# Four of twelve blocks of attention probabilities, turned by VectorE and transfers instead of by TensorE

## What is computed

```python
x = x + 0.5 * ffn(layernorm(x), w_gate, w_up, w_down)
x = x + attn(layernorm(x), gamma, w_qkv, w_out)
x = x + 0.5 * ffn(layernorm(x), w_gate, w_up, w_down)

# ffn:  silu(x @ w_gate.T) * (x @ w_up.T) @ w_down.T, 1024 hidden columns
# attn: rows scaled to unit norm, * 16 * gamma; 16 query heads, 4 key/value heads of 64,
q, k = rotary(q), rotary(k)
sim = einsum('bihd,bjhd->bhij', q / 8, k)        # causal mask
out = einsum('bhij,bjhd->bihd', softmax(sim), v) @ w_out
```

## Time and profile before

| | us |
|---|---|
| median of 3 runs | 595.22 (594.51 to 595.42) |
| the profiled execution | 594.24 |
| its span, first to last instruction | 592.4 |

### The profile page before, as it was taken

The page is one execution under the profiler, slowest core; times in us unless marked ns, Lnnn a source line. Parts: engine busy times, 40 slices in busy tenths (PEclk is TensorE's granted clock), DMA queues, the critical chain, the costliest instruction groups (busy, mean ns, idle before and its releaser), DMA issues.

```text
span 592.4 us, 13551 instructions
## 1 busy us (share of the span) xinstructions
PE 560.4 (95%) x4308; PEld 525.4 (89%) x4308; DVE 435.9 (74%) x1302; ACT 395.0 (67%) x1045; POOL 382.4 (65%) x368
## 2 busy tenths in 40 slices
PE   6889988999999999999999999999999999988997
PEld 2877777989999999999999999999999999777897
DVE  4768886859867795868867695868867696888632
ACT  3564993479736895379826896379926896379722
POOL 0666772887739765696838875686838875476523
PEclk9999998999999999999999999999999999989999
DMA  7410000350006200260005300170004400000000
GB/s 251 141 69 3 1 1 20 83 131 2 19 19 156 56 18 0 62 169 0 18 18 134 79 18 0 41 189 0 18 18 116 96 0 0 18 2 2 1 18 19
DMA packets 28089, 29.68 MB, mean 50 GB/s; under 512 B 2976, under 2 KB 25888, under 8 KB 28064
## 3 DMA queue, kind: packets, MB, share of 16 engines
q1 hardware_dynamic: 28064, 29.37, 19.0%
HBM read 8.39 MB, written 2.10 MB: 18 GB/s over the span
## 4 chain that ended last, share of the span: by engine, by line
PE 59%; ACT 13%; issue 10%; DVE 8%; SPq 5%; POOL 3%; DMA 1%; POOLq 0%; DVEq 0%; ACTq 0%
PE bank L928 40%; PE bank L937 7%; PE bank L1049 5%; ACT probs L528 5%; PE bank L1027 4%; SPq L273 3%; PE bank L1023 2%; SPq L262 2%; ACT hid L555 1%; DVE hid L812 1%; PE bank L923 1%; ACT xn L464 1%; DVE rope_s L700 1%; ACT o_sums L540 1%; DMA q_t<-rotated 1%
## 5 line engine op out<-in xcount | busy, mean ns | idle before, releaser
L381 POOL TENSOR_TENSOR probs<-probs,inv_sum 128x512 f32<-128x512 f32 (+1 forms) x64 | 94.0, 1470 | 43.7 <-DVE inv_sum L789 43.5
L528 ACT ACTIVATE probs<-probs,neg_max 128x128 f32<-128x128 f32 (+1 forms) x256 | 113.1, 450 | 1.6 <-DVE neg_max L779 1.6
L390 POOL TENSOR_TENSOR hid_lo<-hid,hid_hi 128x512 fp32r<-128x512 f32 x64 | 83.8, 1314 | 22.4 <-ACT hid_hi L563 21.6
L928 PE MATMUL bank<-xf_t_hi,gate_hi 128*128 128x256 f32 x256 | 75.2, 294 | 5.3 <-DVE hid L812 2.1
L928 PE MATMUL bank<-down_hi,hid_hi 128*128 128x256 f32 x256 | 72.6, 283 | 1.9 <-POOL hid_lo L390 1.9
L928 PE MATMUL bank<-xf_t_hi,up_hi 128*128 128x256 f32 x256 | 72.1, 282 | 0.0
L400 POOL TENSOR_TENSOR o_t_lo<-o_sums,o_t_hi 128x512 fp32r<-128x512 f32 x32 | 41.8, 1305 | 46.7 <-ACT o_t_hi L547 46.6
L928 PE MATMUL bank<-xf_t_lo,gate_hi 128*128 128x256 f32 x256 | 71.6, 280 | 0.0
L928 PE MATMUL bank<-xf_t_hi,gate_lo 128*128 128x256 f32 x256 | 71.6, 280 | 0.0
L928 PE MATMUL bank<-down_lo,hid_hi 128*128 128x256 f32 x256 | 71.4, 279 | 0.0
L928 PE MATMUL bank<-down_hi,hid_lo 128*128 128x256 f32 x256 | 71.4, 279 | 0.0
(11 more groups left out here) (128 smaller groups left out, 1896.5 us busy)
## 6 DMA issues: line engine op xcount, KB each, us to landing
q_t<-rotated SPq DMA_DIRECT2D x96, 128.0 KB, 2.7
k_t<-rotated_k SPq DMA_DIRECT2D x48, 128.0 KB, 2.7
x_in<-in_x SPq DMA_DIRECT2D x7, 256.0 KB, 2.8
out<-y_out SPq DMA_DIRECT2D x7, 256.0 KB, 2.1
probs<-in_w_qkv SPq DMA_DIRECT2D x4, 384.0 KB, 3.3
probs<-in_w_gate SPq DMA_DIRECT2D x2, 512.0 KB, 6.0
probs<-in_w_up SPq DMA_DIRECT2D x2, 512.0 KB, 6.9
probs<-in_w_down SPq DMA_DIRECT2D x2, 512.0 KB, 5.7
```

The costliest lines, as they stand in the source:

```text
L381: nc.gpsimd.tensor_tensor(part, part, inv_sum[:, slot].unsqueeze(2).broadcast_to([P, GROUP, keys]), ALU.mult).then_inc(p_done, 1)
L390: nc.gpsimd.tensor_tensor(hid_lo[:, slot].rearrange("p c n -> p (c n)"), hid[:, slot], hid_hi[:, slot].rearrange("p c n -> p (c n)").bitca ...
L528: last = nc.scalar.activation(part, part, ACT.Exp, bias=neg_max[:, slot, g:g + 1], scale=-1.0, accum_out=row_sum[:, slot, g:g + 1])
L928: last = nc.tensor.matmul(dst, a[x], b[y], start=start and i == 0, stop=stop and i == 2, skip_group_check=shared)
```

## The change

In the loop, the blocks of key block 0 of groups 4, 5, 6 and 7 (`TURNED`) take another way. VectorE turns each with one instruction that transposes every 32x32 square (`turn_blocks`), into one of two halves of a new buffer `turned`; SyncE issues four transfers for it (`z_restack`), each of which takes 32 partitions of `turned` to all 128 partitions of the low part's buffer, 512 bytes for each; ScalarE copies the block from there to the high part's buffer (`turned_hi`), and VectorE subtracts that in place (`turned_lo`). SyncE's transfers of group n wait for the turned block and for `values(n - 2)`.

The columns of a block then lie by row square, head and row in it. The eight blocks that TensorE still transposes in the loop are written to the bank in the same arrangement (`by_rows`), and `small_half` and `add_large_half` put the sums back in the order of the heads (`head_order`). `values` multiplies key block 1 first and waits for each block by itself. The opening and the ending keep their transposes.

The lists of the loop are new on all engines. They hold the same calls as before, in another order, but for the new ones and those that they replace.

```diff
-TRANSPOSES = dict(opening=22, turn=15, ending=20)
+BLOCK = 32
+TURNED = [(4, 0), (5, 0), (6, 0), (7, 0)]
+TRANSPOSES = dict(opening=22, turn=15 - len(TURNED), ending=20)
...
-        sb("under_rotated_k", [P, 2, 2, SEQ])
+        turned = sb("turned", [P, 2, P // BLOCK, GROUP * BLOCK])
...
+        def head_order(turn, part, bank_order=False):
+
+            if turn.now is None:
+                return part
+            if bank_order:
+                return part.rearrange("p (a g q) -> p a g q", a=P // BLOCK, g=GROUP)
+            return part.rearrange("p (g a q) -> p a g q", a=P // BLOCK, g=GROUP)
...
+        z_ready, z_hi, z_lo = (sig(n, len(TURNED)) for n in ("z_ready", "z_hi", "z_lo"))
+        z_in = [sig(f"z_in{i}", 16 * (P // BLOCK)) for i in range(len(TURNED))]
...
+            def z_restack():
+
+                m = c["Z"]
+                n, kb = TURNED[m]
+                sp.wait_ge(z_ready, turn.at(z_ready, m + 1))
+                sp.wait_ge(rope_sum, turn.at(rope_sum, NT * ROW_JOBS + QK_JOBS))
+                if n > 1:
+                    sp.wait_ge(o_ready, turn.at(o_ready, GROUPS + n - 1))
+                for a in range(P // BLOCK):
+                    sp.dma_start(p_t[n % 2][1][:, kb, a * P:a * P + P].bitcast(F32),
+                                 turned[BLOCK * a:BLOCK * a + BLOCK, m % 2]).then_inc(z_in[m], 16)
+                c["Z"] += 1
...
-                k_restack(0), q_restack(0), k_restack(1), q_restack(1), k_restack(2), q_restack(2), k_restack(3)
-                q_restack(3), x_load(), y_store()
+                k_restack(0), k_restack(1), q_restack(0), q_restack(1), q_restack(2), k_restack(2), k_restack(3)
+                q_restack(3), z_restack(), z_restack(), x_load(), z_restack(), z_restack(), y_store()
...
+            def turned_hi(n, kb):
+
+                m = TURNED.index((n, kb))
+                act.wait_ge(z_in[m], turn.at(z_in[m], 16 * (P // BLOCK)))
+                nc.scalar.activation(p_t[n % 2][0][:, kb], p_t[n % 2][1][:, kb].bitcast(F32), ACT.Copy
+                                     ).then_inc(z_hi, 1)
...
-                nc.scalar.activation(o_sums[rows], bank[O_BANK][other], ACT.Copy).then_inc(o_small, 1)
+                nc.scalar.activation(head_order(turn, o_sums[rows]), head_order(turn, bank[O_BANK][other], True), ACT.Copy
+                                     ).then_inc(o_small, 1)
...
+            def turn_blocks(n, kb):
+
+                m = TURNED.index((n, kb))
+                dve.wait_ge(p_done, turn.at(p_done, GROUPS + n + 1))
+                if m == 0:
+                    for j in range(KV_HEADS):
+                        dve.wait_ge(k_in[j], turn.at(k_in[j], 16 * 2))
+                if m > 1:
+                    dve.wait_ge(z_in[m - 2], turn.at(z_in[m - 2], 16 * (P // BLOCK)))
+                nc.vector.transpose(turned[:, m % 2].rearrange("p b (g q) -> p g b q", g=GROUP),
+                                    probs[:, n % 4, :, kb * P:kb * P + P].rearrange("p g (k b) -> p g b k", b=P // BLOCK)
+                                    ).then_inc(z_ready, 1)
+
+            def turned_lo(n, kb):
+
+                dve.wait_ge(z_hi, turn.at(z_hi, TURNED.index((n, kb)) + 1))
+                rest = p_t[n % 2][1][:, kb]
+                nc.vector.tensor_tensor(rest, rest.bitcast(F32), p_t[n % 2][0][:, kb].bitcast(F32), ALU.subtract
+                                        ).then_inc(z_lo, 1)
...
+                sums = head_order(turn, o_sums[rows])
+                nc.vector.tensor_tensor(sums, sums, head_order(turn, bank[O_BANK][rows], True), ALU.add).then_inc(o_sum, 1)
...
-                first_statistics(), rope_products(0), rope_products(1), row_shift(), second_statistics(x2)
-                rope_products(2), x_lo(xf_t), rope_lo(0), rope_lo(1), rope_products(3), gate_product(), up_product()
-                rope_products(4), gate_product(), up_product(), gate_product(), row_shift(), up_product()
-                mask_max(0), mask_max(1), value_halves(), mask_max(0), mask_max(1), inverse(), gate_product()
-                x_lo(xf_t), up_product(), mask_max(0), inverse(), mask_max(1), mask_max(0), p_lo(0, 0), inverse()
-                mask_max(1), gate_product(), mask_max(0), mask_max(1), inverse(), p_lo(1, 0), add_large_half(0)
-                mask_max(0), inverse(), mask_max(1), add_large_half(1), up_product(), p_lo(2, 0), gate_product()
-                p_lo(3, 0), mask_max(0), up_product(), inverse(), mask_max(1), add_large_half(2), p_lo(4, 1)
-                mask_max(0), p_lo(4, 0), ffn_residual(x1_next, x_in), inverse(), gate_product(), add_large_half(3)
-                p_lo(5, 1), p_lo(5, 0), mask_max(1), up_product(), attention_statistics(), inverse()
-                add_large_half(4), p_lo(6, 1), p_lo(6, 0), add_large_half(5), gate_product(), up_product()
-                p_lo(7, 1), add_large_half(6), p_lo(7, 0), row_shift(True), add_large_half(7), x_lo(xa_t)
-                ffn_residual(y_out, x2), attention_residual(x2, 0), attention_residual(x2, 1)
+                first_statistics(), rope_products(0), row_shift(), rope_products(1), rope_products(2)
+                second_statistics(x2), x_lo(xf_t), rope_lo(0), rope_lo(1), row_shift(), rope_products(3)
+                gate_product(), up_product(), rope_products(4), gate_product(), up_product(), gate_product()
+                mask_max(0), mask_max(1), up_product(), value_halves(), mask_max(0), mask_max(1), gate_product()
+                up_product(), inverse(), x_lo(xf_t), mask_max(0), mask_max(1), inverse(), inverse(), p_lo(0, 0)
+                mask_max(0), mask_max(1), gate_product(), up_product(), mask_max(0), inverse(), p_lo(1, 0)
+                mask_max(1), add_large_half(0), p_lo(2, 0), mask_max(0), mask_max(1), inverse(), add_large_half(1)
+                gate_product(), mask_max(0), mask_max(1), turn_blocks(4, 0), ffn_residual(x1_next, x_in), inverse()
+                add_large_half(2), up_product(), p_lo(3, 0), mask_max(0), turn_blocks(5, 0), p_lo(4, 1), inverse()
+                add_large_half(3), gate_product(), turned_lo(4, 0), mask_max(1), up_product(), turn_blocks(6, 0)
+                inverse(), p_lo(5, 1), add_large_half(4), turned_lo(5, 0), p_lo(6, 1), turn_blocks(7, 0)
+                attention_statistics(), add_large_half(5), turned_lo(6, 0), p_lo(7, 1), gate_product(), up_product()
+                add_large_half(6), turned_lo(7, 0), row_shift(True), add_large_half(7), ffn_residual(y_out, x2)
+                x_lo(xa_t), attention_residual(x2, 0), attention_residual(x2, 1)
...
+                    to = t_bank(c)[:, i * P:i * P + P]
+                    if by_rows:
+                        to = t_bank(c)[:].rearrange("p (a g q) -> p a g q", a=P // BLOCK, g=GROUP)[:, :, i]
+                    last = nc.tensor.transpose(to, block_in, eye_sb[:])
...
-                pe.wait_ge(t_lo, turn.at(t_lo, c[f"p{n % 2}"]))
                 if n == 0:
                     pe.wait_ge(v_done, turn.at(v_done, c["V"]))
                 else:
                     pe.wait_ge(o_sum, turn.at(o_sum, c["O"]))
-                for kb in range(t + 1):
+                for kb in range(t, -1, -1):
+                    if turn.now is not None and (n, kb) in TURNED:
+                        pe.wait_ge(z_lo, turn.at(z_lo, TURNED.index((n, kb)) + 1))
+                    else:
+                        pe.wait_ge(t_lo, turn.at(t_lo, c[f"p{n % 2}"]))
                     for s in range(2):
                         last = nc.tensor.matmul(bank[O_BANK][:], v_halves[:, kb, j], p_t[n % 2][s][:, kb],
-                                                start=kb == 0 and s == 0, stop=kb == t and s == 1)
+                                                start=kb == t and s == 0, stop=kb == 0 and s == 1)
...
-                gate(), scores(0), scores(1), up(), down(), scores(0), gate(), scores(1), up(), x_transposes("ff")
-                scores(0), down(), scores(1), down(), scores(0), gate(), scores(1), p_transposes(0, 0)
-                p_transposes(1, 0), up(), scores(0), values(0), scores(1), gate(), scores(0), scores(1)
-                p_transposes(2, 0), values(1), down(), p_transposes(3, 0), scores(0), scores(1), up(), values(2)
-                p_transposes(4, 1), p_transposes(4, 0), gate(), scores(0), values(3), up(), scores(1)
-                p_transposes(5, 1), p_transposes(5, 0), down(), values(4), p_transposes(6, 1), p_transposes(6, 0)
-                gate(), up(), values(5), down(), p_transposes(7, 1), p_transposes(7, 0), values(6), projection(0, 0)
-                down(), values(7), projection(0, 1), down(), x_transposes("xa"), projection(1, 0), projection(1, 1)
+                gate(), scores(0), scores(1), up(), down(), scores(0), scores(1), gate(), up(), scores(0)
+                x_transposes("ff"), scores(1), down(), down(), scores(0), scores(1), p_transposes(0, 0), gate()
```

(6 more changed lines are left out.)

36 lines of the change are left out of this document (17 added, 19 removed).

## The result

The changed kernel takes **599.8 us** (598.5 to 600.9) beside 595.4 us of the kernel before, both on the same chip: ratio **1.0069**, 95% interval 1.0048 to 1.0091. It is slower by 4.1 us (0.0069 x 595.4). The forecast was 585.0 with a range of 581.5 to 592.0, so both the size and the sign were wrong. The profiled execution took 598.53 us, with a span of 596.7. In what follows runs are compared by their ratios to the kernel before, which ran beside each of them, and a change in us is the difference of two ratios times 595.4; where two runs stood side by side, their times are given too.

A forecast was written before the change was run, and what follows sets the result against it. TensorE, busy 95% of the span, was taken as the bound. -10.3 - 2.0 + 1.2 + 0.9 = -10.2 us took the profiled 594.24 to 584.0; the median, 1.0 above, gave 585.0 us, range 581.5 to 592.

The forecast's parts named there:

- term -10.3: TensorE in the loop: 16 of 48 transposes a turn removed, 1.72 us a turn, -10.3 us over six turns.
- term +0.9: New order in the loop: VectorE's added transposes fit its spare; a tenth or two a turn for mis-walking, +0.9 us.
- I count 0.6 us each: VectorE's four new transposes a turn, 128 partitions x 512 elements: 0.6 us each, 2.4 us a turn.
- rival (a): VectorE's transposes take 1.2 us, half of the additional 2.5 us a turn reaches TensorE: 7.5 us, 592.5; chance 0.10.
- That is 0.04 us a block on an engine that is not the bound: Evictions of turned blocks now read SBUF: VectorE up to 720 for 684 ns, nothing on the path.
- What is moved: Start of a turn: VectorE's first row shift goes behind the first rotary products, TensorE's waits for normalised rows go, -2.0 us.
- I put 0.2 us a turn on that place: At values(7), where the transfer chain and a second chain end with none in hand: 0.2 us a turn, +1.2 us.
- -2.0 for the first shift: Start of a turn: the shift 1.1 us earlier removes TensorE's waits of 0.34 to 0.40 us for normalised rows, -2.0 us.
- rival (b): The transfer chain of the turned blocks does not fit before values(7) and values(4): +8 to +17 us, 593 to 602; chance 0.10.
- The broken output: TensorE's remaining transposes write PSUM in four runs of 32 columns: counted as nothing, ends +5 and -1 us.
- rival d: TensorE's remaining transposes get dearer by 0.1 us a block through their broken output: +5 us, 590; chance 0.05.
- The q transfers: First scores get their q 1.25 us later on SyncE's queue: counted as nothing, at worst q waits double, +1.5 us.

The follow-up runs named there:

- Plain views: Changed kernel with VectorE's four transposes a turn reading and writing runs of 32 elements in order, blocks landing in wrong places: 590.9 us, ratio 0.9937.
- the mended version: Changed kernel, transposes reading 32 neighbouring columns, values reordered by four more transfers a turn, second row shift behind third gate product: 589.3 us, ratio 0.9905.
- the three runs: Kernel before with 12 of 48 TensorE transposes a turn left out (593.0 us), with ScalarE's copies made smaller (595.6), and with both (586.8).

## Why the prediction was wrong, step by step

**"So a microsecond of TensorE's work that is taken out of a turn is a microsecond saved, as long as nothing else becomes late"** (term -10.3): wrong at its condition. The removed work is as counted: 96 transposes are gone, and one that stays takes 273 ns on average, before and after. But ScalarE, 23.33 of 24.00 us busy in the earlier trace rows, was late already when three quarters of it were removed: a third of the 7.8 us came (2.6, from 1.4 to 3.6). The prediction had the number and wrote that ScalarE "has almost none" to spare, and then walked the order as if that cost a tenth or two (term +0.9).

**"I count 0.6 us each, since it reads and writes the same number of elements"**: mis-sized, and the main error. It is 1.11 us, near the upper end of 1.22. Plain views take 0.70 in the kernel, so even for them 0.6 was a tenth too low. The prediction named the strided input as a reason for rival (a) and set it aside with "every other form of VectorE here costs by its element count", but none of those forms has a strided fp32 input from SBUF, so the rows could not say it. Rival (a) was right that the strided transposes are slow and that what stands behind them comes late. Its price, 7.5 us, is near the measured 7.9 by luck: it took a larger addition (0.62 us a transpose, 0.41 measured) and a smaller share of it that reaches TensorE (half, four fifths measured). And it wasn't the slower rival: the 0.10 for slower stood on the transfers, which had no part in it.

**"That is 0.04 us a block on an engine that is not the bound"** (the low part of a turned block): wrong by mechanism. An instruction with two SBUF inputs doesn't run beside one of GpSimd's on SBUF. In the second turn it took 1.17 and 1.44 us beside `normalise()`, against 0.69 alone:

```profile
216.94 1.90 POOL L406 TENSOR_TENSOR probs<-probs,inv_sum 128x1024 f32<-128x1024 f32 x1 [0.97 <-DVE inv_sum L842]
...
218.22 1.17 DVE L744 TENSOR_TENSOR p_even_lo<-p_even_lo,p_even_hi 128x512 fp32r<-128x512 f32 x1
...
219.44 0.50 PE L1110 MATMUL bank<-p_even_hi,v_halves 128*128 128x512 f32 x1 [0.48 <-DVE p_even_lo L744]
```

GpSimd's instruction ends at 218.84, VectorE's 0.55 us later, TensorE's wait as that ends. The wait, 0.48 us, is as long as what the lock adds here (1.17 for 0.69), and yet the wait went with plain views alone. Whether it would also have gone without the lock wasn't tried. `factor` at the end of a turn (in `row_shift(True)`, two SBUF inputs of 128x2) is caught too, at 1.24 us where it took 0.14 before, but TensorE waits for nothing there:

```profile
L703 DVE SCALAR_TENSOR_TENSOR factor<-power_out 128x2 f32<-128x2 f32 x8 | 7.7, 968 | 0.0
```

The trace of the kernel before had the lock already, with the roles changed: the row of 720 ns in the earlier trace rows has two SBUF inputs, and where it ran (246.20 to 246.93 in the third turn) GpSimd's power took 1.47 us instead of the 1.01 of the earlier trace rows:

```profile
246.33 1.47 POOL L324 TENSOR_TENSOR power_out<-power_in,exponent 128x4 f32<-128x4 f32 x1
```

The shift of 0.52 us in the earlier trace rows, for two columns, was another sign. What this lock costs the kernel as a whole was not isolated: the mended version still has it (1.04 us mean for the odd blocks), so it is an open part of the 4.7 us below.

**"What is moved"**: left a step out. The prediction followed the first row shift, rightly, and not the second one, which the same lines move ahead of the first gate product. That cost 3.7 us.

**"I put 0.2 us a turn on that place"** (`values(7)`): right place, too small; 0.63 in the second turn. The statistics and a transpose on VectorE and the output's low part on GpSimd are ahead of it.

**-2.0 for the first shift**: the waits are gone as said. By time -0.8, from -1.9 to +0.4.

**The transfers**, on which rival (b) and most of the care went: right as forecast and without weight. Four issues take 2.5 us and land 2.1 us after the issue; TensorE waits for none of them. **The broken output** costs nothing (rival d: 273 ns for a transpose in both kernels). **The q transfers** cost nothing.

From the forecast to the result, in ratios of runs: 7.9 us for the strided reading, 3.7 for the second shift (together 9.8), and 4.7 us that the mended version stays above 585.0 (589.7 by its ratio, give or take 1.6). The 4.7 us are TensorE's work that buys less: its busy time in that version is 5.3 us under the kernel before's (560.4 to 555.1), where 10.3 were removed. In the kernel before it was ScalarE that took the gain back, which the three runs show; in the changed order it is VectorE and the handovers ahead of it, which is argued.

## What to carry to other kernels

Before work goes to another engine, look at the fullest stretch of a turn and not at the mean: where a second engine is nearly full there (here ScalarE, 23.33 of 24.00 us), removing work from the first buys a part (here a third), and what is added to an engine that becomes full costs most of its length (here four fifths). Price an instruction by its operands, not its element count: where they lie (SBUF or PSUM, one or two) and how far apart their elements are. And follow every instruction that a reordered line carries, on every queue; here two of the losses were a view and a moved line, and both could be mended without giving up the idea.

## What the runs showed of the hardware

- VectorE's 32x32 transpose of 128x512 fp32 takes 0.71 us with neighbours read in order and 1.10 with elements 16 bytes apart. An output that jumps after each 32 elements costs nothing more (0.71), and neither does an instruction of GpSimd beside it.
- VectorE's instructions with two SBUF inputs stand still while GpSimd runs one that reads and writes SBUF: 128x4 in 2.01 us beside 2.07, about 0.1 alone (0.29 for three). A plain fp32 copy in SBUF does so too, 2.28 for 0.42. With one input in PSUM and one in SBUF it stays at 0.69.
- A transfer of 64 KB from SBUF to SBUF takes 0.62 us of SyncE to issue and lands after 2.1 us.
- A wait of 0.24 us inside a run of matmuls shows only as a longer piece of the chain (0.94 becoming 1.18), not as idle time of TensorE.
